# Giving GpSimd the products of six states instead of five in three of eight groups of a selective scan

## What is computed

```python
u = silu(causal_depthwise_conv(xp))                 # 256 channels
dt_r, Bm, Cm = split(u @ W_xp)                      # 8, 16 and 16 columns
delta = softplus(dt_r @ W_dt + dt_bias)
dA  = exp(delta * A)                                # per token, channel, state
dBu = delta * Bm * u
h   = dA_t * h + dBu_t                              # over the tokens
y_t = einsum('ben,bn->be', h, C_t)                  # sum over the 16 states
y = (y + u * D_skip) * silu(z);  y @ W_out
```

## Time and profile before

| | us |
|---|---|
| three runs: median (lowest, highest) | 487.36 (486.67, 488.3) |
| the profiled execution: device time | 486.38 |
| its span, first to last instruction | 484.6 |
| DVE busy | 447.3 (92%) |
| POOL busy | 422.1 (87%) |
| PE busy, its weight loads | 397.5 (82%), 272.7 (56%) |
| ACT busy | 378.3 (78%) |

### The profile page before, as it was taken

How to read it: one execution, slowest core, us unless ns; L and a number is a source line. 1 busy time by engine, 2 the same in 40 slices (tenths; PEclk the granted TensorE clock), 3 DMA queues, 4 the chain that set the end, 5 groups by cost and what they waited for, 6 DMA issues and landing times. The chain is left out here.

```text
span 484.6 us, 6708 instructions
## 1 busy us (share of the span) xinstructions
PE 397.5 (82%) x2133; PEld 272.7 (56%) x2164; DVE 447.3 (92%) x539; ACT 378.3 (78%) x690; POOL 422.1 (87%) x236
## 2 busy tenths in 40 slices
PE   6979775996679887997799888997789787588596
PEld 2546454673547545674557546674657555566374
DVE  6598999989999999999999899989999899999872
ACT  4377985688877998788967998699966997777825
POOL 6149899999999989999899889999999889999910
PEclk8899987999799999999989999999999998799999
DMA  6675027200722018300733018300732027300001
GB/s 160 169 257 206 0 76 299 89 0 1 283 96 83 1 45 331 110 0 2 252 133 99 2 52 323 108 2 0 265 127 93 0 62 313 109 2 22 0 1 43
DMA packets 24146, 51.06 MB, mean 105 GB/s; under 512 B 4521, under 2 KB 14256, under 8 KB 20016
## 3 DMA queue, kind: packets, MB, share of 16 engines
q1 hardware_dynamic: 24112, 50.64, 30.5%
HBM read 48.01 MB, written 2.62 MB: 104 GB/s over the span
## 5 line engine op out<-in xcount | busy, mean ns | idle before, releaser
L606 POOL TENSOR_TENSOR hc<-h,c_rows 128x1024 f32<-128x1024 f32 x127 | 297.8, 2363 | 21.3 <-DVE h L1382 20.8
L1382 DVE TENSOR_TENSOR_SCAN h<-dA,state,dbu 128x512 f32<-128x512 f32 x192 | 233.5, 1263 | 7.3 <-ACT dA L697 7.3
L697 ACT ACTIVATE dA<-delta,a_neg 128x512 f32<-128x512 f32 x256 | 172.8, 685 | 39.6 <-DVE h L1382 39.1
L1123 PE MATMUL yb<-ident,hc 128*128 128x128 f32 x1024 | 151.1, 282 | 20.1 <-POOL hc L606 18.9
L1123 PEld LDWEIGHTS yb<-ident,hc 128*128 128x128 f32 x1024 | 127.6, 146 | 65.7 <-issue 41.0
L1395 DVE TENSOR_TENSOR dbu<-du,bb 128x1024 f32<-128x1024 f32 x88 | 105.3, 1197 | 4.3 <-remote 2.0
L593 POOL TENSOR_TENSOR dbu<-du,b_rows 128x1024 f32<-128x1024 f32 x40 | 94.5, 2363 | 4.5 <-DMA b_rows<-bc_dram 4.5
L1382 DVE TENSOR_TENSOR_SCAN h<-dA,dbu 128x512 f32<-128x512 f32 x64 | 74.0, 1203 | 2.8 <-ACT dA L697 2.6
L1023 PE MATMUL mf<-f_hT,w_conv 128*128 128x512 f32 x112 | 53.3, 599 | 2.0 <-ACT zu L757 1.4
L1148 PE MATMUL bb<-b_parts,sel 128*128 128x512 bf16 x63 | 25.1, 398 | 30.9 <-DVE dbu L1395 29.6
L1148 PEld LDWEIGHTS bb<-b_parts,sel 128*128 128x128 bf16 x88 | 8.7, 99 | 47.4 <-DVE dbu L1395 27.3
(11 more groups left out here) (206 smaller groups left out, 512.2 us busy)
## 6 DMA issues: line engine op xcount, KB each, us to landing
c_rows<-bc_dram SPq DMA_DIRECT2D x32, 1024.0 KB, 7.7
b_rows<-bc_dram SPq DMA_DIRECT2D x40, 256.0 KB, 8.7
xs<-in_L_attn_x_dram SPq DMA_DIRECT2D x8, 256.0 KB, 3.7
out_dram<-xs SPq DMA_DIRECT2D x7, 256.0 KB, 5.6
ygT<-in_L_attn_conv_w_dram SPq DMA_DIRECT2D x2, 256.0 KB, 4.2
bc_dram<-xd SPq DMA_DIRECT2D x8, 64.0 KB, 1.6
w_in<-in_L_attn_W_in_dram SPq DMA_DIRECT2D x2, 128.0 KB, 4.0
probT<-in_L_wmod_dram SPq DMA_DIRECT2D x1, 256.0 KB, 4.0
```

Of the source, the lines that this page charges most:

```text
L606: nc.gpsimd.tensor_tensor(hc[:, pair % RC, :, :], h[:, pair % RH, :, :], c_rows[:, q, n % NQ, :].unsqueeze(1).broadcast_to([P, HALVES, T]) ...
L697: nc.scalar.activation(dA[ke % RD][:, :], delta[:, ge % 2, half, :], ACT.Exp, scale=a_neg[:, half, n:n + 1]).then_inc(s_dA, 1)
L1123: last = nc.tensor.matmul(bank[:, tile], hc[:, pair % RC, half, tile], ident[:, :], start=False, stop=n == N - 1, is_transpose=True, skip_ ...
L1382: v.tensor_tensor_scan(h[:, pair % RH, half, :], dA[k % RD][:, :], dbu[:, pair % RW, half, :], start, ALU.mult, ALU.add).then_inc(s_scan, 1)
```

## The change

In groups 1, 2 and 3 POOL makes dbu of states 2, 5, 7, 9, 11 and 14; in the others of 2, 5, 8, 11 and 14, as before. State 8 goes from POOL to DVE, states 7 and 9 from DVE to POOL, in each of the three groups. `b_rows` gets a sixth row, and the counters that engines wait on are made from lists by group. Since a row of `b_rows` now serves other states in other groups, SP waits for the last dbu that read that row.

```diff
-    POOL_N = (2, 5, 8, 11, 14)
-    NB = len(POOL_N)
+    POOL_N = tuple((2, 5, 7, 9, 11, 14) if 1 <= g < 4 else (2, 5, 8, 11, 14) for g in range(GROUPS))
+    NB = max(len(states) for states in POOL_N)
...
         def by_pool(pair):
 
-            return pair // N * NB + sum(n < pair % N for n in POOL_N)
+            g = pair // N
+            return sum(len(states) for states in POOL_N[:g]) + (sum(n < pair % N for n in POOL_N[g]) if pair % N else 0)
+
+        def is_pool(pair):
+
+            return pair % N in POOL_N[pair // N]
+
+        def row_loads(i, g):
+
+            return sum(len(states) > i for states in POOL_N[:g + 1])
...
-                        if n in POOL_N:
-                            i = POOL_N.index(n)
+                        if n in POOL_N[f]:
+                            i = POOL_N[f].index(n)
                             if g >= 0:
 
-                                sp.wait_ge(s_pdbu, g * NB + i + 1)
+                                last = max(g2 for g2 in range(f) if len(POOL_N[g2]) > i) if row_loads(i, g) else None
+                                if last is not None:
+                                    sp.wait_ge(s_pdbu, by_pool(last * N + POOL_N[last][i]) + 1)
...
-                        pool.wait_ge(s_bld[i], 16 * (gd + 1))
+                        pool.wait_ge(s_bld[i], 16 * row_loads(i, gd))
```

More of the change, by code:

```diff
@@ L584, in _ @@
                     pair = (g * STEPS + s) // HALVES + AHEAD_POOL
-                    if s % HALVES == HALVES - 1 and 0 <= pair < PAIRS and pair % N in POOL_N:
+                    if s % HALVES == HALVES - 1 and 0 <= pair < PAIRS and is_pool(pair):
                         gd, n = divmod(pair, N)
-                        i = POOL_N.index(n)
-                        pool.wait_ge(s_bld[i], 16 * (gd + 1))
+                        i = POOL_N[gd].index(n)
+                        pool.wait_ge(s_bld[i], 16 * row_loads(i, gd))
                         pool.wait_ge(s_du, HALVES * (gd + 1))
@@ L1135, in _ @@
                     kf, ks = k + AHEAD_FILL, k - LAG_SUM
-                    if 0 <= kf < K and kf % HALVES == 0 and kf // HALVES % N not in POOL_N:
+                    if 0 <= kf < K and kf % HALVES == 0 and not is_pool(kf // HALVES):
                         pair = kf // HALVES
@@ L1368, in _ @@
                         if half == 0:
-                            if n in POOL_N:
+                            if n in POOL_N[g]:
                                 dve.wait_ge(s_pdbu, by_pool(pair) + 1)
@@ L1384, in _ @@
                     kd = k + AHEAD_DBU
-                    if 0 <= kd < K and kd % HALVES == 0 and kd // HALVES % N not in POOL_N:
+                    if 0 <= kd < K and kd % HALVES == 0 and not is_pool(kd // HALVES):
                         pair = kd // HALVES
```

## The result

| | before | after |
|---|---|---|
| median (lowest, highest), us | 487.71 (486.67, 488.3), 4 runs | 491.37 (490.79, 493.1), 4 runs |
| ratio, 95% interval | | 1.0079 (1.0058 to 1.0099) |
| profiled execution, its span | 486.38, 484.6 | 493.1, 491.0 |

The change costs 3.85 us by the ratio (the medians differ by 3.66), by its interval 2.8 to 4.8. A fourth run of the kernel before has moved its median from 487.36 to 487.71. The changed kernel is slower by more than 0.3%, as forecast; the forecast time was 491.9, its loss 4.55.

The account below looks back on a forecast made before the run. In groups 2 and 3 neither DVE nor POOL alone bounds, but a loop of waits through POOL, PE, ACT and some DVE scans; POOL has no slack in group 1. 2.33 + 2 x 1.11 = +4.55, 487.36 + 4.55 = 491.9 us; range 489.0 to 494.4.

Parts of the forecast that it names:

- Group 1, +2.33: POOL in group 1: a sixth dbu where POOL has no idle time, so hc 15 ends 2.33 us later.
- Groups 2 and 3, +1.11 each: DVE's new dbu of state 8 between scans 14 and 15, on the path: 1.11 us more in each group.
- A: Part of the period from scan 13 to hc of state 10, over DVE and ACT; 14.58 us before the change.
- C: Part of the period from the end of hc 15 to the next group's scan 13, over PE and ACT; 18.33 us.
- B: Part of the period from hc 10 to the end of hc 15, POOL practically without a gap; 21.39 us.
- POOL's sixth dbu in groups 2 and 3, 0: POOL from hc 15 to hc 10: 32.62 us of work against 32.91 over the scans, so no cost.
- DVE without the dbu of states 7 and 9, 0: DVE before scan 13 and after scan 16: removed work turns into waiting for ACT's dA, so no gain.
- Groups 4 to 7 as before: After group 3 everything keeps its old distance from hc 15; these groups only come 4.55 us later.
- the loop: Waits from hc 15 to scan 13, to hc 10, to the next hc 15: 18.33 + 14.58 + 21.39 = 54.30 us, the period.
- DVE is the bound: Rival, DVE's busy time: three dbu less on DVE save 3.3 us, giving 484.0; chance 0.05.
- PE's clock: Rival, PE after hc 15: longer waits place a half-clock stretch on the path, 493.6 for one; chance 0.06.

Follow-up runs that it names:

- states 7 and 8: Kernel before, groups 2 to 6: POOL makes dbu of 2, 5, 7, 8, 11, 14 (state 7 added, state 8 kept); 0.9995, -0.2 us.
- the experiment at equal work: Kernel before, groups 2 to 6: state 7 to POOL and state 8 to DVE, five states on POOL as before; 1.0127, +6.2 us.
- state 3 for 2: Kernel before, groups 1 to 7: POOL makes dbu of 3, 5, 8, 11, 14, state 3 in place of 2; 0.999, -0.5 us.
- half of du: Kernel before, first half of du of the next group moved on POOL from step 25 to step 19; 1.0000, 0.0 us.
- both halves: Kernel before, both halves of du of the next group moved on POOL to steps 19 and 20; 1.0015, +0.7 us.
- the fourth: Kernel before, POOL makes dbu of 1, 4, 8, 11, 14 in groups 4 to 6, first half of du moved to step 19; 0.9982, -0.9 us.

## Why the prediction was right

- **Group 1, +2.33.** Measured +2.31, and +2.31 again where it was done alone (54.02 to 56.33). POOL had no gap, and scan 13 of group 2 came 18.25 after hc 15. DVE waited 0.76 us for du (forecast 0.8), and it was covered as worked out.
- **Groups 2 and 3, +1.11 each.** A grew by 1.14 and 1.12. The mechanism holds to the row: scan 16 4.68 after scan 13 (forecast 4.7), scan 20 13.17 (13.15), 1.40 idle before it (1.4). The net of the groups was 0.89 and 1.34, since other parts differed: in group 2 C by -0.08 and B by -0.16, in group 3 C by +0.23. That these cancel, so that the three groups add up to 4.54 for 4.55, is luck.
- **POOL's sixth dbu in groups 2 and 3, 0.** Right: POOL idled 1.33 and 1.57 before hc 10, and with state 8 left on POOL still 0.28.
- **DVE without the dbu of states 7 and 9, 0.** Right; the idle time before scan 13 grew to 1.72 in group 2 (forecast over 1.4), and to 1.33 in group 3, a little less than forecast.
- **Groups 4 to 7 as before.** Right for 5 to 7. Group 4 was 0.67 shorter, all in C. It is as large as the 0.7 us between 4.55 forecast and 3.85 measured, but it comes from one profile of each kernel, and the interval takes in both. The granted clock, and PE in group 4, in the profiles before and after:

```profile
243.20:246.60 3.40, 3.40 (x10) 2.07 (x11) 3.40 (x4) 1.50 (x3) 3.40 (x3) 0.51 0.76 312
...
252.91 1.25 PE L1123 MATMUL yb<-ident,hc 128*128 128x128 f32 x8
254.00 1.45 PE L1023 MATMUL mf<-f_hT,w_conv 128*128 128x512 f32 x3
```

```profile
250.20:253.70 3.50, 3.19 (x14) 1.67 (x15) 3.50 (x4) 2.44 (x4) 3.50 (x3) 1.00 0.80 330
...
259.82 0.65 PE L1134 MATMUL yb<-ident,hc 128*128 128x128 f32 x4 [0.42 <-POOL hc L617]
```

  Before, PE did 10 products in 3.40 busy us at half clock, until 6 us before the end of hc 15, and was late when it came: it worked off 8 transposes and went on with `xp` at 254.00, 1.26 after 252.74. After, at full clock, it did 14 in 3.19, and idled 0.42 for hc 15, with `xp` 0.54 behind it. So C of group 4 was 0.7 longer before than the loop needs. In three other kernels (group 1 alone, groups 2 and 3 alone, state 9 added) C of group 4 was 18.79, with a half-clock stretch of 3.4 us that ended 4.8 to 5.7 us before hc 15. In two (state 7 for 8, states 7 and 8) the last such stretch had ended over 25 us before, and C was 18.26. That the clock makes the difference fits all seven profiles; it wasn't isolated.

- **The rivals.** "DVE is the bound" fell by the sign and by the experiment at equal work. The rule of the Trainium skill ("Perfetto Trace Analysis", Identifying the Most-Contended Engine), to optimise the engine with the highest occupancy first, did not hold here: DVE led with 92%, three dbu fewer on it went with +3.85 us, and five fewer with 0, where none changed its place on DVE (state 9 or 7 added on POOL). "PE's clock" didn't come as a loss; it moved the other way, in group 4.
- **What was incomplete.** The prediction said that DVE's work before scan 13 is beside the path. For a loss that holds: hc 15 later by 2.31 made everything 2.31 later. For a gain it does not: in group 5 DVE's scans of states 0 to 5 reach scan 13 by ACT's dA and copies only 0.04 us sooner than hc 15 does. In groups 3 and 6 they come last already. The prediction tested its 18.3 in groups 2, 3 and 5; in group 6 C was 18.69 before the change too, with these rows of ACT and PE:

```profile
370.19 0.69 ACT L697 ACTIVATE dA<-delta,a_neg 128x512 f32<-128x512 f32 x1 [0.47 <-DVE h L1382]
...
371.54 1.16 PE L1034 MATMUL mf<-w_in,f_hT 128*128 128x128 f32 x8 [0.69 <-ACT zu L757]
```

  PE waits 0.69 for the copy behind that dA, where it waited 0.25 in group 5; the 0.44 more are the 18.69 less 18.25. In group 3 of the changed kernel the same dA comes 9.05 us after hc 15 by a wait for DVE, before it was 8.82: that is the +0.23 of its C. The test of the prediction, that C stays 18.3 whether DVE idles 0.2 or 1.54 before scan 13, could not see that, as DVE's late work (statistics, state 7) isn't on this second path and its early work is. The change itself only lengthens paths, so no more than this 0.23 came of it; the first three attempts to shorten one (state 3 for 2, half of du, both halves) were mis-forecast by 2 to 3 us, the fourth by 1.5.

## What to carry to other kernels

Read a periodic kernel as a loop: find the waits that lead from one group to the next, add up the distances, and place each moved instruction in one of them; the busy shares told nothing of the cost here, as the same work in another place made 1.13 us a group. Here an instruction ahead of a wait was free and the same instruction behind it was paid in full. A closed loop is proof for a delay, not for a saving: before forecasting a gain, look for the next path, which shows as a wait that another engine still has in the same stretch (here ACT's 1.61 us for DVE's scans). An edit that shortens one path must be checked on the others: states 1 and 4 on POOL took time off DVE's way and put 0.5 to 0.6 us on POOL's.

## What the runs showed of the hardware

**The clock of the program's start differs between executions.** The same stretch in the profiles of before and after:

```profile
29.00:38.00 9.00, 6.31 (x27) 3.35 (x27) 8.73 (x9) 6.45 (x15) 5.88 (x4) 1.00 1.01 388
```

```profile
29.00:38.00 9.00, 7.09 (x23) 4.03 (x22) 7.92 (x8) 5.69 (x13) 5.02 (x4) 0.62 1.02 380
```

With a granted clock of 0.62 instead of 1.00 of full (2.4 GHz; the part at half, 1.2 GHz, was 31.0 to 37.8) PE did 23 products for 27. Scan 0 to scan 13 of group 0 took 24.11 us in three of twelve profiles (before, group 1 alone, states 7 and 8), 25.80 in three (groups 2 and 3 alone, state 9 added, both paths) and 26.50 to 26.58 in six. The half clock lasted 0, 3.4 and 6.8 us there. No edit touches what the compute engines do between these two scans. In 26 runs of the kernel before alone the mean granted clock lay between 0.947 and 0.968: the four runs at 0.947 took 487.8 to 489.3 us, the two at 0.968 took 485.4 and 485.8. Such differences of 2.4 us, 0.5% of the time, are more than most effects here, and only medians or a stretch without the start show those.

**A half-clock stretch on the path costs as much as a change.** Between groups 0 and 1, in the kernel before and in the one with states 1 and 4 alone:

```profile
82.80:86.20 3.40, 2.79 (x10) 2.28 (x11) 3.40 (x4) 1.51 (x3) 3.40 (x3) 0.50 0.00 0
```

```profile
84.20:91.00 6.80, 6.14 (x18) 3.88 (x18) 6.80 (x7) 2.33 (x5) 6.80 (x4) 0.50 0.02 9
```

Where it lasted 6.8 us and reached up to hc 15, C of group 1 was 19.68 instead of 18.25, and POOL idled 0.99 before hc 10 where it had not idled at all: group 1 took 55.06 instead of 54.02. The kernel with state 7 for 8 shows the same (stretch at 84.1, group 55.09), and so does that with states 7 and 8 (half clock from 68.0 to 88.5, 1.3 us before hc 15, group 54.81). Where the last stretch ended 3.7 us or more before hc 15, in eight other profiles, C was 18.24 to 18.26 (the kernel with state 3 for 2 has another C and is left aside). What makes the stretch longer wasn't tried.

**No sign that POOL and DVE disturb each other.** In the kernel before, all 192 scans of the form with a start state took 1250 to 1284 ns and all 127 hc 2329 to 2388 ns, over the whole program. In the changed kernel DVE's scan has a mean of 1266 ns (1263 before) and POOL's 43 dbu one of 2371 ns (2363 for 40).
